# Hand-written orders of work on five engines for a gated cross-attention and ternary feed-forward layer

## The reference

```
h  = layernorm(x)                                   # ln1
q, k, v = h @ Wq.T + bq, ctx @ Wk.T + bk, ctx @ Wv.T + bv
p  = softmax(clip(mask(q k / sqrt(32))))            # 16 heads, 512 x 64
d  = layernorm(rs * (p v @ Wo.T + bo)) * gamma + beta
x1 = x + tanh(g_xattn) * d
n  = layernorm(x1)                                  # then rounded to 8 bits per token
a  = silu(bitlin(n, gate_w) + gate_b) * (bitlin(n, val_w) + val_b)
y  = x1 + tanh(g_ffn) * (bitlin(a, out_w) + out_b)
```

## Time and profile before

| | us |
|---|---|
| median of 3 runs (lowest, highest) | 716.33 (715.44, 716.71) |
| the profiled execution | 714.52 |
| its span, first to last instruction | 712.7 |
| PE busy | 665.8 (93%) |
| DVE busy | 586.1 (82%) |
| ACT busy | 497.7 (70%) |
| POOL busy | 311.1 (44%) |

### The profile page before, as it was taken

One profiled execution on the slowest core, in us unless ns is written; L12 is line 12 of the kernel. 1 busy time (PEld: TensorE's weight loads), 2 busy tenths in 40 slices (PEclk: granted clock), 3 DMA queues, 4 the chain that ended last, 5 costly groups with the idle time before them and its releaser, 6 DMA issues.

```text
span 712.7 us, 14015 instructions
## 1 busy us (share of the span) xinstructions
PE 665.8 (93%) x4555; PEld 320.1 (45%) x4566; DVE 586.1 (82%) x1226; ACT 497.7 (70%) x660; POOL 311.1 (44%) x483
## 2 busy tenths in 40 slices
PE   4899656979999999999999999999999999999997
PEld 4435435434444454445444544454444444454444
DVE  5888798887877977898888887888779877879986
ACT  3487789679657975787668767786579656964444
POOL 2310315234644465445635473456535643363530
PEclk9999885999999999999999999999999999999999
DMA  9884545031742356236543545336433731363212
GB/s 328 236 283 158 121 184 160 4 74 39 152 113 68 84 132 136 62 77 127 115 97 88 118 103 118 88 84 137 100 75 75 162 75 44 61 127 93 64 45 75
DMA packets 170231, 79.84 MB, mean 112 GB/s; under 512 B 149385, under 2 KB 149713, under 8 KB 169554
## 3 DMA queue, kind: packets, MB, share of 16 engines
q1 hardware_dynamic: 170194, 79.37, 45.4%
HBM read 37.59 MB, written 10.56 MB: 68 GB/s over the span
## 4 chain that ended last, share of the span: by engine, by line
PE 37%; DVE 28%; issue 16%; POOL 6%; DMA 5%; ACT 5%; another core or an unknown queue 1%; SPq 1%; DVEq 0%; POOLq 0%; ACTq 0%
PE psum L1843 11%; PE psum L1906 9%; PE psum L1897 6%; PE psum L1972 4%; DVE arena L1309 3%; DVE hmax L1314 2%; ACT arena L928 2%; DVE xmax L1394 2%; DVE stats L1382 2%; DMA arena<-arena 2%; DMA arena<-x_both 2%; DMA arena<-in_L_xattn_Wq 2%; DVE arena L1412 1%; POOL arena L699 1%
## 5 line engine op out<-in xcount | busy, mean ns | idle before, releaser
L1843 PE MATMUL psum<-ternary,xqT 128*128 128x512 f16 x1024 | 240.2, 383 | 0.0
L1843 PEld LDWEIGHTS psum<-ternary,xqT 128*128 128x128 f16 x1024 | 95.0, 99 | 117.8 <-issue 14.6
L888 ACT ACTIVATE arena<-psum,dequant 128x512 f32<-128x512 f32 x128 | 86.5, 681 | 45.6 <-PE psum L1843 31.9
L1897 PE MATMUL psum<-ternary,arena 128*128 128x512 f16 x496 | 116.1, 379 | 2.4 <-DMA arena<-arena 2.4
L691 POOL TENSOR_TENSOR rstd<-var_e,minus_half 128x1 f32<-128x1 f32 x64 | 40.1, 626 | 162.0 <-DVE var_e L1360 85.5
L1309 DVE SCALAR_TENSOR_TENSOR arena<-psum,dequant,arena 128x512 f32<-128x512 f32 x105 | 78.1, 744 | 13.2 <-ACT arena L888 11.9
L1906 PE MATMUL psum<-wo_hi,arena 128*128 128x512 f16 x256 | 81.4, 379 | 2.0 <-ACT arena L943 1.9
L1314 DVE TENSOR_REDUCE hmax<-arena 128x1 f32<-128x1024 f32 x64 | 77.6, 1212 | 0.5
L1906 PE MATMUL psum<-arena,wq_hi 128*128 128x512 f16 x256 | 76.2, 379 | 1.2 <-DMA arena<-x_both 0.8
L1897 PEld LDWEIGHTS psum<-ternary,arena 128*128 128x128 f16 x496 | 45.9, 98 | 59.4 <-issue 9.7
L928 ACT ACTIVATE arena<-arena,round_c 128x1024 f16<-128x1024 f32 x62 | 70.9, 1144 | 0.6 <-DVE arena L1333 0.6
(11 more groups left out here) (211 smaller groups left out, 1175.3 us busy)
## 6 DMA issues: line engine op xcount, KB each, us to landing
arena<-in_x SPq DMA_DIRECT2D x64, 256.0 KB, 2.8
out<-arena SPq DMA_DIRECT2D x31, 256.0 KB, 2.3
arena<-in_L_ffn_gate_w SPq DMA_DIRECT2D x4, 1024.0 KB, 12.2
arena<-in_L_ffn_out_w SPq DMA_DIRECT2D x4, 1024.0 KB, 5.1
ternary<-in_L_ffn_val_w SPq DMA_DIRECT2D x2, 1024.0 KB, 10.8
arena<-arena SPq DMA_TRANSPOSE x90, 3.1
ternary<-in_ctx SPq DMA_DIRECT2D x1, 1024.0 KB, 5.5
ternary<-in_L_xattn_Wk SPq DMA_DIRECT2D x1, 1024.0 KB, 8.1
```

The lines of the kernel that those rows point to most:

```text
L888: A.activation(gs[:, t % 2, n * CW:(n + 1) * CW], psG[n % 2], ACT.Silu, scale=dequant[:, t, 0:1]).then_inc(silu_done.sem, 1)
L1843: ins = M.matmul(ps[:], xqT[:, t % 2, k, :], w[:, k, cols], start=(not begun and k == 0), stop=(k == KC - 1 and i != 2))
L1897: ins = M.matmul(psO[:], hidT[t % 2][:, k, :], wo2[:, k, :], start=(k == 0), stop=(k == FC - 1))
```

## The change

All lists keep their calls; what changes is their order. On each engine the setup, `first_row`, `first_tile` and `second_tile` are rearranged, and the loop body gets a written list (`if prev and ffn and att and pre:`) in place of the nest, which stays for the last two tiles of row 0 and for rows 6 and 7. The PE lists, and of the others the parts that the prediction speaks of:

```diff
 # SP, setup: gate_w after the loads of x for row 1; load_w(1, 3) before the biases
-            for c in range(W_CHUNKS):
-                load_w(0, c)
             for t in range(2):
                 sp.wait_ge(s_h0_tr, t + 1)
                 sp.dma_start(xa[:, t, :], x[1, ...]).then_inc(xa_loaded[t].sem, 16)
+            load_w(0, 0)
...
             load_w(1, 2)
+            sp.wait_ge(s_pe, TURN["values", KC - 1] + 1)
+            load_w(1, 3)
             sp.wait_ge(s_bpart, PARTS)
...
             load_keys(0)
+            for t in range(2):
+                sp.dma_start(xres[:, t, :], x[0, ...]).then_inc(xt_loaded[t].sem, 16)
# SP, loop body
+                    normed_x(c, 0)
+                    load_keys(a)
+                    residual_x(b, 2)
+                    store(b - 1, 2)
+                    normed_x(c, 1)
+                    hidden_T(b - 1, 3)
+                    hidden_T(b, 0)
+                    residual_x(b, 3)
+                    normed_x(c, 2)
+                    residual_x(a, 0)
+                    store(b - 1, 3)
+                    h_T(c, 0)
+                    wait_alone(sp, s_met_sp, pv_done, a - 1, NT)
+                    load_values(v_dram.rearrange("(b t) n -> b t n", t=T)[a])
+                    h_T(c, 1)
...
# PE, first_row (from project(0, 0))
                     project(0, 0)
-                    first_c_transpose(2)
+                    weight_total(1)
                     first_c_transpose(3)
                     wait(pe, c_ready, 0, NT)
-                    for g in range(SETUP_BANKS):
-                        weight_transpose(0, g)
+                    weight_transpose(0, 0)
...
+                    weight_transpose(1, 5)
                     wait(pe, d_ready, 0, 1)
                     project(0, 1)
-                    weight_total(1)
-                    xq_transpose(0, 0)
-                    for g in range(SETUP_BANKS, W_GROUPS):
-                        weight_transpose(0, g)
-                    for g in range(W_GROUPS):
-                        weight_transpose(1, g)
+                    weight_transpose(1, 6)
+                    weight_transpose(1, 7)
# PE, second_tile
                     project(0, 2)
+                    weight_transpose(2, 4)
+                    weight_transpose(2, 5)
                     gate_val(1, 0)
-                    weight_transpose(2, 4)
                     gate_val(1, 1)
-                    weight_transpose(2, 5)
+                    gate_val(1, 2)
                     weight_transpose(2, 6)
-                    gate_val(1, 2)
                     weight_transpose(2, 7)
                     gate_val(1, 3)
...
                     down(0, 0, range(0, DOWN_AT_SCORES[1]))
+                    down(0, 0, range(*DOWN_AT_SCORES[1:]))
                     scores(1)
-                    down(0, 0, range(*DOWN_AT_SCORES[1:]))
# PE, loop body
+                    project(b, 1, with_bo=False)
+                    gate_val(0, 0)
+                    gate_val(0, 1)
+                    query(0)
+                    query(1)
+                    query(2)
+                    query(3)
+                    gate_val(0, 2)
+                    gate_val(0, 3)
+                    down(b - 1, 3, range(0, 8))
+                    xq_transpose(b, 1)
+                    project(b, 2, with_bo=False)
+                    gate_val(1, 0)
+                    gate_val(1, 1)
+                    down(b - 1, 3, range(8, 16))
+                    gate_val(1, 2)
+                    gate_val(1, 3)
...
+                    down(b, 1, range(0, 12))
+                    down(b, 1, range(12, 16))
+                    xq_transpose(b, 3)
# DVE, first_row (its end)
                     weight_copy(1, 3)
+                    weight_copy(1, 5)
                     weight_round(1, 3)
-                    weight_copy(1, 5)
+                    weight_sum(2)
                     weight_copy(1, 7)
# ACT, first_row: sum_abs(1, 1) from the setup to after query(1), round_w(0, 0) to before query(0)
# ACT, loop body, tiles 0 and 1
+                    inverse_rows(b, 1)
+                    h_high(c, 0)
+                    quant(b, 0)
+                    silu(1, 0)
+                    hidden_codes(b, 0, 0)
+                    silu(1, 1)
+                    hidden_codes(b, 0, 1)
+                    norm(c, 1)
+                    result(b - 1, 3)
# ACT, loop body, tile 3
+                    round_input(a, 0)
+                    norm(c, 3)
+                    silu(3, 2)
+                    h_high(c, 2)
+                    h_high(c, 3)
+                    silu(3, 3)
# POOL, loop body
+                    root(b, 2, 1)
+                    update_inverse(b, 2)
+                    result(b - 1, 3)
```

More of the change, by code:

```diff
@@ L561, in body @@
                     h_T(1, 3)
-                    for t in range(2):
-                        normed_x(2, t)
-                    sp.dma_start(valb_b[:, :], bcast(val_b[F - CW:], CW)).then_inc(s_vbias, 16)
+                    normed_x(2, 0)
+                    normed_x(2, 1)
+                    return
+                if prev and ffn and att and pre:
+                    normed_x(c, 0)
[13 more added lines that the diff above has]
+                    h_T(c, 1)
+                    normed_x(c, 3)
+                    hidden_T(b, 1)
+                    residual_x(a, 1)
+                    c_T(a, 0)
+                    c_T(a, 1)
+                    c_T(a, 2)
+                    store(b, 0)
+                    store(b, 1)
+                    hidden_T(b, 2)
+                    c_T(a, 3)
+                    h_T(c, 2)
+                    h_T(c, 3)
                     return
@@ L1172, in _ @@
             values(2)
-            sum_abs(1, 1)
             values(3)
-            for k in range(KC):
-                high("wq", 0, k, wq_hi)
+            high("wq", 0, 0, wq_hi)
+            high("wq", 0, 1, wq_hi)
+            high("wq", 0, 2, wq_hi)
+            high("wq", 0, 3, wq_hi)
             rows(act, body)
@@ L1511, in first_tile, with second_tile @@
+                    hidden(0, 3)
                     hidden_max(0, 0)
-                    weight_copy(2, 2)
+                    hidden_max(0, 1)
                     weight_clip(2, 2)
-                    hidden(0, 3)
+                    hidden_scale(0)
                     xq_T(0, 1)
                     q_low(1, 2)
+                    q_low(1, 3)
+                def second_tile():
+                    weight_clip(2, 3)
+                    statistics(True, True, 0, 2, 1)
+                    hidden(1, 0)
+                    hidden(1, 1)
+                    x_shift(2, 1)
+                    weight_copy(2, 4)
+                    new_x(0, 2)
+                    weight_copy(2, 6)
+                    x1_stats(0, 2)
+                    input_scale(0, 2)
+                    hidden(1, 2)
+                    hidden(1, 3)
+                    hidden_max(1, 0)
+                    hidden_max(1, 1)
+                    bound(0)
+                    bound(1)
+                    hidden_scale(1)
+                    xq_T(0, 2)
+                    bound(2)
+                    bound(3)
@@ new lines, in body @@
+                if b is FIRST:
+                    first_row()
+                    return
+                if prev and ffn and att and pre:
+                    statistics(True, True, b, 1, 0)
+                    x_shift(c, 0)
+                    hidden(0, 0)
+                    q_low(a, 0)
+                    new_x(b, 1)
+                    hidden(0, 1)
+                    hidden_max(0, 0)
+                    x1_stats(b, 1)
+                    input_scale(b, 1)
+                    q_low(a, 1)
+                    q_low(a, 2)
+                    hidden(0, 2)
+                    hidden(0, 3)
@@ L1517, in first_tile @@
                     hidden_max(0, 1)
                     hidden_scale(0)
-                    weight_clip(2, 3)
-                    q_low(1, 3)
-                def second_tile():
-                    statistics(True, True, 0, 2, 1)
+                    xq_T(b, 1)
+                    statistics(True, True, b, 2, 1)
+                    new_x(b, 2)
                     hidden(1, 0)
-                    new_x(0, 2)
-                    x_shift(2, 1)
-                    weight_copy(2, 4)
+                    x_shift(c, 1)
@@ L1537, in second_tile @@
                     bound(0)
+                    xq_T(b, 2)
                     bound(1)
-                    xq_T(0, 2)
                     bound(2)
                     bound(3)
-                if b is FIRST:
-                    first_row()
+                    statistics(True, True, b, 3, 2)
+                    attention_out(0)
+                    hidden(2, 0)
+                    new_x(b, 3)
+                    x_shift(c, 2)
+                    hidden(2, 1)
+                    attention_out(1)
+                    x1_stats(b, 3)
+                    hidden_max(2, 0)
```

(21 more changed lines are left out.)

342 lines of the change are left out of this document (236 added, 106 removed).

## The result

The changed kernel takes 704.58 us (median of 4 runs, 703.26 to 705.21) against 715.88 (714.04 to 716.71) for the kernel before beside it: ratio 0.984, 95% interval 0.9814 to 0.9865. I had forecast 714.3, with 711.0 to 718.5 as the range. So the sign was right, and the gain of 11.3 us was over five times my 2.0. The profiled execution took 704.56, its span 702.7 (712.7 before).

A forecast was written before the change was run, and what follows sets the result against it. PE was taken to bound the kernel, busy 93%, with the idle time in the prologue. Prologue -2.3 and loop +0.3 gave -2.0 us: 714.3 on the median of 716.33, range 711.0 to 718.5.

The forecast's parts named there:

- The loop is at PE's floor: Loop body: 73.69 of a row's 74.5 us is PE work, so five rows hold at most 4 us.
- +0.06 a row: Loop body: the new order costs 0.06 us a row, +0.3 in all; bounds -0.3 and +1.2 a row.
- The six margins: Loop body: six new places, numbered (1) to (6), all hold without a wait, by 0.2 to 2 us.
- (6): Loop, SP: load_values behind store(b-1, 3) still lands in time, at 320.2 against 322.05 where weighted(0) wants the values.
- The rival of late values: Loop: values land late for weighted(0) since SP waits for POOL's result; 0.9 us a row, 718.5 us; chance 0.22.
- Setup: Start of the kernel to about 62 us: the new order changes nothing, 0 us, bounds -0.6 to +3.
- first_row: Prologue up to the end of gate_val(0, 0): +1.2 for a later start, -1.8 for the clock, sum -0.6 us.
- Full clock for `gate_val(0, 0)`: Prologue, first gate_val: runs at full clock, 1.90 instead of 3.44 us; with its bias products -1.8 us.
- the +1.2: Prologue: gate_val(0, 0) starts 0.8 to 1.4 us later, behind DVE's copies and weight_round(1, 3); taken as +1.2.
- The idle 3.4 at weight_total(1): Prologue, first_row: PE idles some 3.4 us waiting for sum_abs(1, 3), at no cost in time.
- first_tile and second_tile: Prologue, first two tiles of row 0: shorter stalls and a full-clock gate_val(1, 2), -3.9 at scores(0), -2.0 us net.
- a new wait of 1.2 at `weighted(0)`: Prologue, row 1 of the list: weighted(0) waits 1.2 us for d_ready behind hidden_max, bound and statistics on DVE.

The follow-up runs named there:

- e13: Changed prologue with the loop's order of before on all engines, and on PE gate_val(0, 1) moved ahead of query(0): 706.05 us.
- e14: Changed prologue with the loop's order of before, and on PE the last four products of down(b, 1) moved ahead of xq_transpose(b, 3): 707.08 us.
- e2: Changed kernel, but in the loop only PE keeps its new list; the other four engines have the order of before: 730.65 us.
- e3: Changed kernel, but in the loop PE has the order of before; SP, POOL, ACT and DVE keep their new lists: 721.35 us.
- e5: Changed kernel, but ACT has the order of before in the loop: 744.90 us.
- e6: Changed kernel, but DVE has the order of before in the loop: 719.40 us.
- e7: Changed kernel, but SP has the order of before in the loop: 710.16 us.
- e8: Changed kernel, but in the loop PE interleaves the four gate_val(0, i) with query(i) again: 717.10 us.
- e10: Changed kernel with first_row of before on all engines: 706.14 us.
- e12: Changed kernel, but PE does project(0, 1) at its old place, right behind the fourth weight_transpose: 707.16 us.
- e11: Changed kernel with first_tile and second_tile of before on all engines: 707.12 us.
- e18: Changed prologue with the loop's order of before on SP, ACT, DVE and PE, and POOL's new list: 729.97 us.

## Why the prediction was wrong

**The loop is at PE's floor: false.** This is the step that failed most. I read 73.69 busy of 74.5 as a floor, called the rest gaps between modelled ends, and counted only the named 0.30, though the same view had two lines more, at `query(0)` and `project(b, 1)`. My own bound for the five rows, 4 us, was exceeded: they gave 4.8. The trace had the 1.01 in the starts of five products, and e13 and e14 took two of these gaps away by one move each. Instead of +0.06 a row it was -0.99.

**The six margins: right.** None of (1) to (6) shows a wait. With a partner's list put back or moved, waits of 0.4 to 2.2 us came up (e2, e3, e5 to e8). The values (6) are tighter than my 1.85 us: `result(b-1, 3)` ends at 305.83, the loads are issued from 308.35, the last of the four at 310.78, and each lands 2.1 to 2.2 us after its issue. So the last is there at 312.9, 1.1 before `weighted(0)` at 314.03 (timelines of POOL, SP's queue and DVE, after, to be held against the earlier trace rows):

```profile
304.56 1.27 POOL L752 TENSOR_TENSOR arena<-arena 128x512 f32<-128x512 f32 x1
```
```profile
308.35 3.03 SPq L528 DMA_DIRECT2D vcur<-v_scratch  x4
```
```profile
313.05 0.74 DVE L1496 SCALAR_TENSOR_TENSOR delta<-psum,mv,gamma_b 128x512 f32<-128x512 f32 x1
```

`weighted(0)` still waits for that last instruction, d_ready. The rival of late values didn't come about.

**Setup, 0 forecast (and +0.3 of small shifts in the sum), about -1.1 measured.** The keys are waited for nowhere, as I said. What I left out is that PE's two waits for `row_max` shrink from 1.6 to 0.7 us. It lies beyond my bound of -0.6, and the one trace after hides it behind its half-clock stretch.

**first_row, -0.6 forecast, -2.1 measured (e10).** Full clock for `gate_val(0, 0)`: right in size and, by e12, in cause. The clock rose behind a run of transposes again, as I took from the earlier trace rows against the Trainium skill (TensorE: Matmul & The Clock Gate, Part 4: PE-mode transpose); in 112.0 to 115.5 transposes alone kept PE full at 0.50, the 16 transposes at 115.89 took 1.06 us, full speed, and 1.00 was granted in 116.7 to 119.7. The wrong term is the +1.2 by which `gate_val(0, 0)` was to start later: against row -1's `weighted(0)` it starts 0.5 earlier. Two parts of it: the last transposes ran at full clock (1.05 for 1.87), which I had left out, and weight_round(1, 3) ended 0.5 late and not 1.2, since I had taken DVE's durations as fixed. Before, three of its passes ran beside POOL's tensor operations (timeline of DVE, before, then after):

```profile
111.43 2.18 DVE L1227 TENSOR_SCALAR extra<-extra 128x2048 f32<-128x2048 f32 x1
...
114.13 1.58 DVE L1232 TENSOR_SCALAR ternary<-ternary 128x2048 f32<-128x2048 f32 x1
```
```profile
111.44 1.23 DVE L1357 TENSOR_SCALAR extra<-extra 128x2048 f32<-128x2048 f32 x1
...
113.78 1.22 DVE L1362 TENSOR_SCALAR ternary<-ternary 128x2048 f32<-128x2048 f32 x1
```

**The idle 3.4 at weight_total(1): right in size**, 3.60. That it has no price wasn't tried by itself.

**first_tile and second_tile, -2.0 net forecast, -4.6 measured (e11).** The gain up to `scores(0)` was well sized: -3.9 forecast; from the start of `gate_val(0, 0)` to `scores(0)` it is 34.32 us after and 38.70 in e11, -4.4. What failed is the 1.8 I let be given back: a new wait of 1.2 at `weighted(0)` measured 0.22, and ACT's 0.6 didn't appear, `scores(0)` to `weighted(0)` being 10.77 after and 10.91 before.

In sum the forecast, 714.3, missed by 9.7, and its gain of 2.0 by 9.3. In the trace it was 8.0 of span: 5.1 in the loop, 3.9 in the prologue, less the 1.0 given back at the end. With the half-clock stretch of the setup in neither trace the prologue's share would be about 5.7.

## What to carry to other kernels

A full PE in the windows view is not a floor: measure from start to start against the pitch of its products, for a stall that is mostly under a product's drawn tail is in no list of waits, and five places made 1.4% of this loop. Orders on several engines are one object: one list alone (PE, DVE, POOL) or all but one (PE, ACT, DVE, SP) cost 1 to 8 us a row, so a list is judged with its partners, and single moves (e13, e14) are what can be tried alone. Independent products just ahead of a stretch that needs the full clock can be worth more than their own time. Before a part of the change is given a price from one trace of each kernel, look for half-clock stretches that only one of them has: here one hid 1.7 us.

## What the runs showed of the hardware

- **DVE slows beside POOL.** `new_x` (two 128x512 f32 operands) takes 0.74 to 0.75 us by itself and 1.59 to 1.73 where a POOL tensor operation of 128x512 had begun 0.1 to 0.2 us before it; where POOL's began 0.3 us after it, it took 0.75. For `q_low` it is 0.68, and 1.38 to 1.54 where POOL's had begun 0.3 before. Means over four rows, before and then after (groups by line and shape: busy, mean ns):

```profile
L1376 DVE SCALAR_TENSOR_TENSOR delta<-delta,rstd,arena 128x512 f32<-128x512 f32 x16 | 22.8, 1426 | 0.0
```
```profile
L1505 DVE SCALAR_TENSOR_TENSOR delta<-delta,rstd,arena 128x512 f32<-128x512 f32 x16 | 11.9, 746 | 0.1
```

The Trainium skill (SBUF — State Buffer, SBUF: two separate sides) states such a rule: a DVE operation with two SBUF inputs and a GpSimd operation that reads SBUF lock a shared pair of ports against each other, and the later one blocks until the other is through. The rows agree, also in which of the two is held.

The lists keep the two apart, and DVE's busy time of a row falls from 62.1 to 59.4 us. Since DVE wasn't the bound, this bought time only where a chain ran through it.

- **The clock in a hole.** Behind 3.33 us of idle PE (e12) the granted clock was 0.50, that is 1.2 GHz, and both the transposes (1.86 us) and the first eight products (3.59 us) ran at that. Behind 2.36 us in e18, with PE busy 1.84 of the 4.2 us before, it was 0.50 too (13 products in 4.67 us); behind 2.52 us in another row of the same trace they took 2.98, full speed. So a wait of PE can be paid a second time, and not always.
